# Another written-down order for the attention half of a two-layer transformer kernel, with first attention steps among the q/k/v products and joint diagonal units

## The reference, cut to what matters

```python
x = _layernorm(x + _L0_attn_ref(x))      # a 256x256 softmax mix of features
x = _layernorm(x + _L0_ffn_ref(x, ...))  # gated MLP, LoRA of 2 of 8 experts per token
x = _layernorm(x + _L1_attn_ref(x, L1_attn_w_qkv, L1_attn_w_o))
x = _layernorm(x + _L1_ffn_ref(x, ...))  # 32 small experts, top 8, kept up to 0.8

# _L1_attn_ref
qkv = jnp.einsum('bsh,oh->bso', hidden_states, w_qkv)      # 16 heads of 16
scores = jnp.einsum('bhqd,bhkd->bhqk', q, k) * scale
scores = jnp.where(causal, scores, jnp.finfo(scores.dtype).min)
probs = jax.nn.softmax(scores, axis=-1)
attn = jnp.einsum('bhqk,bhkd->bhqd', probs, v)
return jnp.einsum('bsh,oh->bso', attn, w_o)
```

## Time and profile before

| | us |
|---|---|
| median of 3 runs | 1606.34 |
| lowest, highest | 1599.44, 1610.54 |
| the profiled execution: its time | 1600.74 |
| its span (first to last instruction) | 1599.0 |
| PE busy in the span | 1464.6 (92%) |
| DVE busy | 936.7 (59%) |
| ACT busy | 627.5 (39%) |
| mean granted TensorE clock | 0.91 |

### The profile page before, as it was taken

How to read it: one execution, slowest core, us unless ns; L and a number is a source line. 1 busy time by engine, 2 the same in 40 slices (tenths; PEclk the granted TensorE clock), 3 DMA queues, 4 the chain that set the end, 5 groups by cost and what they waited for, 6 DMA issues and landing times.

```text
span 1599.0 us, 20300 instructions
## 1 busy us (share of the span) xinstructions
PE 1464.6 (92%) x7956; PEld 1043.3 (65%) x7956; DVE 936.7 (59%) x1777; ACT 627.5 (39%) x884; POOL 262.4 (16%) x343
## 2 busy tenths in 40 slices
PE   6689999999999889999999999888889999999995
PEld 5578778788788655344443443454478888888885
DVE  3555753754745457678758878763345545575445
ACT  3032322422322212466546656545523444444331
POOL 3220110200200001012111211301011222232221
PEclk9699999999999865699869999977889999999998
DMA  6000000000000438002400600000001111111110
GB/s 267 0 1 1 1 1 1 0 1 1 20 1 27 149 119 117 1 2 35 46 2 5 77 2 1 21 10 1 1 21 40 45 45 50 50 41 50 50 57 27
DMA packets 31831, 55.41 MB, mean 35 GB/s; under 512 B 6392, under 2 KB 13304, under 8 KB 31224
## 3 DMA queue, kind: packets, MB, share of 16 engines
q1 hardware_dynamic: 29688, 53.85, 13.6%
q0 software_dynamic: 2048, 0.27, 0.2%
HBM read 43.21 MB, written 10.49 MB: 34 GB/s over the span
## 4 chain that ended last, share of the span: by engine, by line
PE 79%; DVE 14%; ACT 4%; issue 3%; POOL 0%; DMA 0%; POOLq 0%; DVEq 0%; ACTq 0%
PE ps L1449 50%; PE ps L1647 9%; PE ps L1717 9%; PE ps L1695 4%; DVE mpart L1236 4%; PE ps L1666 1%; DVE x L1039 1%; PE ps L1471 1%; PE ps L1456 1%; PE ps L1502 1%; ACT probs L940 1%; PE ps L1487 1%; PE ps L1726 1%; PE ps L1513 1%; DVE mpart L1246 1%
## 5 line engine op out<-in xcount | busy, mean ns | idle before, releaser
L940 ACT ACTIVATE probs<-ps 128x1024 f32<-128x1024 f32 (+3 forms) x320 | 277.6, 896 | 238.2 <-PE ps L1695 237.2
L1449 PE MATMUL ps<-xtd,gu 128*128 128x512 f32 x1152 | 283.5, 401 | 7.8 <-DVE x L1279 4.8
L1236 DVE TENSOR_REDUCE mpart<-ps 128x1 f32<-128x512 f32 x384 | 238.0, 682 | 49.8 <-PE ps L1647 49.6
L1647 PE MATMUL ps<-stack 48*128 48x512 f32 (+3 forms) x832 | 232.9, 425 | 36.3 <-DVE mpart L1236 21.0
L1449 PEld LDWEIGHTS ps<-xtd,gu 128*128 128x128 f32 x1152 | 216.3, 191 | 58.8 <-issue 9.8
L1647 PEld LDWEIGHTS ps<-stack 48*128 48x128 f32 x832 | 129.2, 213 | 180.4 <-DVE mpart L1236 110.2
L1449 PE MATMUL ps<-ma,b 128*128 128x512 f32 x672 | 169.0, 401 | 10.3 <-DVE x2f L1185 7.4
L1695 PE MATMUL ps<-stack 50*128 50x512 f32 (+3 forms) x640 | 171.0, 449 | 5.5 <-ACT probs L940 5.4
L1717 PE MATMUL ps<-probs,vaug 128*32 128x512 f32 (+3 forms) x1280 | 172.8, 617 | 1.9 <-POOL probs L820 1.6
L1449 PEld LDWEIGHTS ps<-ma,b 128*128 128x128 f32 x672 | 126.9, 191 | 44.1 <-DVE x2f L1185 10.7
L1449 PEld LDWEIGHTS ps<-dn,hpart 128*128 128x128 f32 x1152 | 144.3, 189 | 5.3 <-DVE hpart L1020 1.0
(11 more groups left out here) (175 smaller groups left out, 1676.9 us busy)
## 6 DMA issues: line engine op xcount, KB each, us to landing
gu_raw<-in_wgu SPq DMA_DIRECT2D x48, 256.0 KB, 2.6
stack<-qk_dram SPq DMA_DIRECT2D x72, 128.0 KB, 9.1
qk_dram<-qk_out SPq DMA_DIRECT2D x16, 512.0 KB, 2.9
dn_raw<-in_wdn SPq DMA_DIRECT2D x48, 128.0 KB, 2.7
stack<-qk_dram SPq DMA_DIRECT2D x48, 64.0 KB, 2.4
x<-in_x_tm SPq DMA_DIRECT2D x4, 512.0 KB, 5.1
xt_in<-in_x_fm SPq DMA_DIRECT2D x1, 2048.0 KB, 8.4
out<-x SPq DMA_DIRECT2D x4, 512.0 KB, 3.1
```

What stands on the lines that cost most here:

```text
L940: act.activation(probs[:, (2 * r + p) % 4, :, off:BLK], banks(bank)[:, :, off:BLK], ACT.Exp, scale=float(HD) ** -0.5).then_inc(exp_done.se ...
L1236: ins = dve.tensor_reduce(part[:, p, qt % TPB, 2 + kb:3 + kb], ps[:, bank, :], AX_X, ALU.max)
L1449: mm = pe.matmul(out, lhs(i), rhs(k), start=first and n == 1, stop=last and n == todo, **more)
L1647: return pe.matmul(out, stack[lo:lo + KROWS, g % 2, 0, b, p, P * t:P * (t + 1)], stack[lo:lo + KROWS, g % 2, 1, kb, p, k0:k0 + width], sta ...
```

## The change

The planner is gone. `ORDER`, a string of letters, gives the second half's order up to the experts; the plan is read off it. Each letter takes the next entry of its kind: `q` a q or k product, `V` values, `T` turnC, `L` `R` `N` the last LoRA output, its residual and norm, `u` a unit, `S` an `st`, `P` a `pv` (with `ucopy` after a round's last), `M` `max` and `maxc` together, `O` `out` and `head` together, `a` to `e` turnO, proj (with resC), normC, turnD, logit, and others for the gate's steps and weights. `maxc` and `head` now stand right behind their transposes for VectorE too, where up to two units stood between.

```diff
+ORDER = (
+    "qqTLRqqVNuuuTuuuVuuquVMuuTuuuquuquuquuVuSuuSuSuuSuPuuuPSuuuSuuMuuuPuuuSuuuuuuSuSuuuuuuuuuuPuuuuuuSuuuSSuuPuSuS"
...
+    "PSuSSuSuuPwdPMeerSSOSwSPSaPSSbSPSsfkSPcSSPSSPSSPSSPSSmPSSPSSPSdPSSSPSSPSSPxe"
+)
...
-        mine = [("diag", g, qb, i, a) for i in range(2) for a in range(2)] + [("half", g, qb, 0, a) for a in range(2)]
...
+        units += [("diag", g, qb, i) for i in range(2)] + [("half", g, qb, 0, a) for a in range(2)]
...
+    taken = {"pair": itertools.cycle((0, 2)), "one": itertools.cycle((4, 5, 7))}
...
+        elif letter == "u":
+            u = units[n]
+            if u[0] == "diag":
+                plan.append(("unit", u, (next(taken["one"]), next(taken["one"]))))
...
-        wqkv = at("wqkv", [P, 2, NC, 3 * H], F32R, R)
-        assert cursor[0] <= R + NT * H * 4
+        wqkv = at("wqkv", [P, 2, NC, 3 * H], F32R, S0 + 2 * HP * T * 4)
...
                     sp_.wait_ge(ones_ready, 1)
-                    for i in range(2):
-                        ones_rows(i)
+                    ones_rows(0)
+            sp_.wait_ge(*v_ps.after(NB - 1))
+            sp_.wait_ge(*qk_ps.after((NB - 1, 1)))
+            ones_rows(1)
...
             def head_out(n, bank):
                 g, qb = rounds[n]
                 dve.wait_ge(*u_turned.after(n))
+                if n:
+                    dve.wait_ge(*o_ready.after(n - 1))
...
+            def diagonal(u, bank):
+
+                _, g, qb, i = u
...
+                for a in range(2):
+                    bank_free(pe, "unit", u + (a,))
+                for n, (p, t) in enumerate([(p, 2 * i + t) for p in range(HP) for t in range(2)]):
+                    for a in range(2):
+                        score(ps[:, bank[a], P * n:P * (n + 1)], a, g, p, qb, t, qb, P * t, P, n == 0)
+                for a in range(2):
+                    pe.matmul(ps[:, bank[a], :], identb[:, :], trimax[:, None, :].broadcast_to([P, TPB, P]),
+                              start=False, stop=True, skip_group_check=True).then_inc(scored.sem, 1)
```

312 lines of the change are left out of this document (81 added, 231 removed).

## The result

| | before | after |
|---|---|---|
| median of 4 runs each, on the same chip, us | 1608.44 | 1527.25 |
| lowest, highest | 1599.44, 1619.82 | 1526.66, 1532.06 |
| ratio, with its interval | | 0.950 (0.943 to 0.956) |
| the profiled execution: time, span | 1600.74, 1599.0 | 1527.2, 1525.5 |
| mean granted clock in it | 0.910 | 0.930 |

What follows compares the result with a forecast made beforehand. In the middle TensorE and VectorE alternate as the limit, neither full, with half clock at its start. Terms -8 - 9 - 10 + 4.5 + 6 - 7 = -23.5 from 1600.74 us gave 1577, put at 1578; range 1550 to 1604.

Steps and rivals of the forecast that it cites:

- terms 4 and 5: Fourth to last `max`: more `pv` and `st` done there, +4.5 us; values closer behind their exps make TensorE wait, +6.
- term 3: Diagonal units made in pairs: 0.3 us gained for each of 32 pairs, -10 us; bounds nothing and 21.
- sign of being wrong: Wrong if the middle moves beyond its bounds (about 386 us; shorter by over 15: freed middle) or the start gains under 10.
- Terms 1 and 2: Two units instead of six between the last products, -8 us; steps put among units before the fourth `max`, -9.
- the second rival: Middle gives back the start's gain through late exps, joint units holding two banks, runs of units: about 1600 us; chance 0.20.
- the first rival: Middle frees itself: units spread so banks are free, a third of 80.5 us of waits goes, 27 us: 1551; chance 0.15.
- Waits as signs: Values' waits for exps over 15 us; pair about 1.2; first step 570 to 580, third `max` 623, fourth 675.
- Term 6: After the last `max`: five steps less, one more logits, one set of transposes less; together -7 us, bounds -10 and -4.
- Term 7: The new wait in `head_out` and the later load of the second half's rows of ones: no cost.
- The rival: Slower clock: runs of units hold TensorE at half clock another 160 us, losing 45 us: 1622; chance 0.08.
- side remark: If the first half-clock hold of 56.5 us in attention vanishes, 16 us are gained, less half-price gains already counted: 1564.

## Why the prediction was wrong, point by point

The direction was right. The sum started from the profiled execution and said -23.5; the profiled execution of the changed kernel is 73.5 us quicker. Of the 50 us between, 27 are time at half clock: the sum took the clock of the trace before as given and had no term for it. The other 23 are at equal clock, and the step that failed there is the middle, terms 4 and 5, with the wrong sign; after it comes the size of term 3. The prediction's own sign of being wrong is met: the middle was to stay at 386 us and not to be shorter by over 15, and it is shorter by 25.3.

- **Terms 1 and 2, the start (-8 and -9).** The sum nearly held (14.3 for 17), but only since two errors cancel. The products alone give 14.3 us at equal clock (the first term is 6 too small: it added up the largest waits of the earlier trace rows, 8.6 us, where all the idle time of TensorE up to the first step was 16.7 and all but 2.7 of it went). The steps among units gave nothing that is seen beyond that: the second term's 9 us were not there. A part of them is the new wait of 4.17 us for the maxima at 589.28; the rest isn't traced.
- **Term 3, joint diagonals (-10).** A pair takes 1.13 us, where 1.15 was estimated. The worth was mis-sized: 0.3 each was taken, 0.52 each measured (16.7 us). The prediction had the places the wrong way round, 0.54 in a row of diagonals and less elsewhere: two pairs directly behind each other take 1.86 us and gain nothing, and in the new order 29 of the 32 pairs have something else directly behind them (`st`, values, half units, once a product). The Trainium skill (TensorEngine Tiling, PSUM Bottleneck) says that packing speeds TensorE up and not the reading of PSUM; the trace agrees for the back-to-back pairs, the second of which waits 0.66 us for the reduce, and not for the others. What was feared under the second rival, VectorE standing still while a pair holds two banks, does occur in the old order (1.17 us idle, then 1.75 us of wait at the place shown, and 3.7 us lost in all).
- **Terms 4 and 5, the middle (+4.5 and +6).** This is the step that failed at equal clock. With single diagonals the new middle has 4.5 us more work (an estimate of the prediction, not tested) and takes 6.3 less, so its order frees some 10.8 us where it was to cost 6. TensorE's idle time there says the same, 29.7 us before and 18.5 with this order. Term 5 is wrong: values nearer to their exps cost nothing. The argument against the first rival ("the new order is less even") counted how many units stand between two values and not where: 76 of the 124 `pv` of the middle have a unit directly ahead of them on TensorE, 43 of 120 before (77 and 55 if a transpose between isn't counted). The runs put 0.17 to 0.19 us on such a place, so 22 to 33 more give 4 to 6 us by estimate. The other 5 to 7 us are not attributed. So the rival "the middle frees itself" was the right one, with some 10.8 us freed by the order where it assumed 27; the joint units come on top (354.9 to 343.0 in the table of stretches). The raw stretch is 25.3 us shorter, past the 15 that were given as its sign.
- **Waits as signs.** Waits of values for exps were to grow from 10 to over 15 us and are 7.3 (9.7 with those under PE; term 5 falls by this too). A pair of 1.13 us (1.2 given) held. The third `max` was to come at 623 and came at 612.6, the fourth at 675 and came at 660.6, the first step at 570 to 580 and came at 558.6, earlier by 10 to 21 us.
- **Term 6, the end (-7).** With no half-clock time 56.2 became 46.5, so -9.7, inside the bounds given; the raw stretch is 50.5 against "near 60".
- **Term 7.** Nothing seen: no unit is listed as waiting for a load of `stack`, and the experts take 453.1 for 451.9.
- **The clock.** The rival had it slower, and as a side remark up to 16 us faster. It gave 27 us in the profiled executions (74 us less at half clock, of which 44 before the fourth `max`: 109 to 65) and 34.8 over all runs (96 us less). Two sizes were off: the time and the price, 0.28 from the earlier trace rows where 0.363 was measured over 176 runs. The row counted values issued in equal stretches; whole programs lose more. That the half-clock time would fall was not foreseen by the sum, and why it does isn't known.

At equal clock the forecast of -23.5 stands against -46.3: 6.7 more from joint units (16.7 for 10), 14.3 more from the middle with its end (forecast +3.5, measured -10.8), 4.5 that only the whole new order has (29.6 - 14.3 - 10.8, most of it behind the last `max`: 50.6 to 46.5 in the table of stretches), and 2.7 less from the start (14.3 for 17). That adds up to the 22.8 between the two.

No kernel of these is faster than the changed one by more than a measurement can tell (1524.91 with 27 more units ahead of values, but an even span 1.2 us longer).

## What to carry to other kernels

When two engines take turns on a few banks, look at what stands directly ahead of the long instruction, and not only at how evenly the entries are spread. An entry that the other engine must read, put just ahead of it, was worth 0.17 to 0.19 us a place here, until most places had one. A quicker way of making two results at once holds two banks at once, and in these runs its gain appeared only with other work behind it, so count what follows it before pricing it. A forecast that takes the clock of the trace before as given can miss by more than all its other terms. Put executions of one kernel to an equal time at half clock before reading effects of a few us; here that took the 72 runs of the kernel before from a range of 66 us to one of 5.

## What was not expected of the hardware

- Time at half clock costs 0.36 us for each us here, and it varied between 230 and 410 us from run to run of the same program, 66 us of span.
- Half clock held with TensorE listed busy for all of 46.00 us, and more matmuls in the units, on 48 rows or on all, didn't raise it. The Trainium skill (TensorE: Matmul & The Clock Gate, What's actually happening) says that activity releases the throttle; in these windows the trace doesn't show it.
- The order changes the half-clock time without adding a matmul: with joint units 303 us in the old order, 286 with the new start alone, 245 with the new middle, 216 with both; with single ones 312, 277 (products), 287 (middle), 242 (all). The differences from end to end are clear; the means of four or five runs (286, 245, 242) are uncertain by 12 to 30. By what it does so isn't known from these runs.
